# Keys kept once with two diagonal rows per key tile, and the projection products in three float32r terms, in a post-norm attention block

## What is computed

```python
qkv = x @ in_proj_weight.T + in_proj_bias          # split into q, k, v; heads of 16
qh = qh / 4
scores = einsum('bhid,bhjd->bhij', qh, kh)
rel = clip(j - i, -64, 64) + 64                    # i: query, j: key
bias = (qh @ rel_pe.T) taken at rel
attn = softmax(scores + bias)
y = layernorm(x + (attn @ vh) @ out_w.T + out_b)
out = layernorm(y + gelu(y @ binarized(w1).T + b1) @ binarized(w2).T + b2)
```

## Time and profile before

| | |
|---|---|
| median of 3 runs | 2366.7 us (2362.38 to 2367.46) |
| time of the profiled execution | 2361.56 us |
| its span, first to last instruction | 2359.6 us |
| mean granted TensorE clock | 0.978 of full speed |
| busy: PE / DVE / ACT / POOL | 94% / 74% / 67% / 46% of the span |
| projection stage, about | 0 to 217 us |
| attention stage, about | 217 to 2005 us |
| feed-forward stage, about | 2005 to 2359 us |

### The profile page before, as it was taken

How to read it: one execution, slowest core, us unless ns; L and a number is a source line. 1 busy time by engine, 2 the same in 40 slices (tenths; PEclk the granted TensorE clock), 3 DMA queues, 4 the chain that set the end, 5 groups by cost and what they waited for, 6 DMA issues and landing times. The chain is left out here.

```text
span 2359.6 us, 47824 instructions
## 1 busy us (share of the span) xinstructions
PE 2227.5 (94%) x14580; PEld 1261.9 (53%) x14580; DVE 1739.1 (74%) x3447; ACT 1573.1 (67%) x2192; POOL 1085.8 (46%) x1803
## 2 busy tenths in 40 slices
PE   8996899999999999999999999999999998899997
PEld 5563444444444444444444444444444443688886
DVE  4443777777777777777777777777777772788885
ACT  3433377777777777777777777777777776466766
POOL 1001444554445544455445545454554431567663
PEclk9998599999999999999999999999999999899999
DMA  9997777777777777777777677777777752333421
GB/s 305 400 352 265 204 208 202 210 214 211 206 207 208 208 213 209 210 203 208 212 209 212 201 208 215 209 208 202 210 213 209 209 178 73 100 102 111 111 65 45
DMA packets 334570, 468.55 MB, mean 199 GB/s; under 512 B 89797, under 2 KB 262550, under 8 KB 334486
## 3 DMA queue, kind: packets, MB, share of 16 engines
q0 software_dynamic: 120960, 215.78, 33.9%
q1 hardware_dynamic: 204358, 243.32, 32.7%
q10 hardware_dynamic: 9168, 8.52, 1.1%
HBM read 244.73 MB, written 221.25 MB: 197 GB/s over the span
## 5 line engine op out<-in xcount | busy, mean ns | idle before, releaser
L933 ACT ACTIVATE probs<-weigh_ps 128x1024 f32<-128x1024 f32 x1024 | 1048.9, 1025 | 471.8 <-PE weigh_ps L1100 468.0
L985 DVE CUSTOM_DVE_ANT_1 ring_ps<-ring_ps,band_all 128x512 f32<-128x512 f32 x1008 | 681.0, 716 | 263.8 <-PE ring_ps L1061 263.6
L1061 PE MATMUL ring_ps<-keys,queries 48*128 48x512 f32 x2048 | 827.1, 468 | 40.1 <-DVE partial_max L974 14.0
L1100 PE MATMUL weigh_ps<-queries,keys 50*128 50x512 f32 (+3 forms) x2688 | 751.0, 385 | 1.3 <-ACT probs L933 0.6
L974 DVE TENSOR_REDUCE partial_max<-ring_ps 128x2 f32<-128x1024 f32 x512 | 627.7, 1226 | 112.3 <-PE ring_ps L1061 80.8
L1061 PEld LDWEIGHTS ring_ps<-keys,queries 48*128 48x128 f32 x2048 | 370.7, 187 | 524.7 <-issue 398.9
L1117 PE MATMUL sum_ps<-probs,values 128*32 128x512 f32 x4096 | 546.6, 605 | 0.1
L839 POOL COPY carried<-carried 128x252 f32<-128x252 f32 x430 | 159.3, 396 | 568.2 <-ACT carried L922 568.2
L1085 PE MATMUL weigh_ps<-ident,band_all 128*128 128x128 f32 x2048 | 363.2, 290 | 19.3 <-ACT carried L922 16.5
L1100 PEld LDWEIGHTS weigh_ps<-queries,keys 50*128 50x128 f32 x2688 | 356.3, 186 | 14.9 <-ACT probs L933 9.5
L1085 PEld LDWEIGHTS weigh_ps<-ident,band_all 128*128 128x128 f32 x2048 | 213.6, 141 | 249.9 <-ACT probs L933 104.6
(11 more groups left out here) (119 smaller groups left out, 1857.3 us busy)
## 6 DMA issues: line engine op xcount, KB each, us to landing
band_scr<-carried SPq DMA_DIRECT2D x256, 512.0 KB, 4.8
band_all<-band_scr POOLq DMA_DIRECT2D x128, 512.0 KB, 5.4
band_all<-band_scr POOLq DMA_DIRECT2D x128, 256.0 KB, 4.4
keys<-k_scr POOLq DMA_DIRECT2D x128, 240.0 KB, 8.1
k_scr<-k_parts SPq DMA_DIRECT2D x16, 1792.0 KB, 9.8
q_scr<-q_parts SPq DMA_DIRECT2D x16, 1024.0 KB, 10.4
queries<-q_scr POOLq DMA_DIRECT2D x128, 128.0 KB, 3.8
o_scr<-weighted_s SPq DMA_DIRECT2D x64, 256.0 KB, 7.6
```

Source lines behind the costliest of these rows:

```text
L933: nc.scalar.activation(probs[:, u % PROBS], weigh_ps[weigh_of["scores", at]][:], ACT.Exp).then_inc(s_pr, 1)
L985: nc.vector.tensor_tensor_reduce(out=both, in0=both, in1=bias, scale=1.0, scalar=LOWEST, op0=ALU.add, op1=ALU.max, accum_out=partial_max[: ...
L1061: nc.tensor.matmul(dst, query_rows(c, h, ROWS, tile * P, (tile + 1) * P), key_rows(c, h, ROWS, c0, c0 + 512), start=True, stop=True, tile_ ...
L1100: last = nc.tensor.matmul(weigh_ps[weigh_of["scores", at]][:, h, e0 * P:e1 * P], key_rows(c, h, QROWS, k0, k0 + P), query_rows(c, h, QROWS ...
```

## The change

Four things are done.

1. Keys are stored once (`KCOLS` of 9 tiles in place of 15), with the left end, except tile 0's first 64 keys and the copy of tile 0 behind tile 7. A new small projection gives, for every head and query, the query times (right end minus left end): `wdT` are its weights, `d_parts` its two float32r parts, `d_scr` its DRAM copy. In `d_scr` each of six key tiles has two rows, zero except over the query tiles for which the right end applies. `load_ends` puts these 12 rows below the three terms of the queries; the keys get 12 fixed rows (`beyond`), ones where the key tile is theirs. A look product has 60 rows, a score product 62 and always 512 columns.
2. All products of the projection stage are made from two float32r parts in three terms: `wT` and `xT` have a second part, computed by DVE.
3. To make room, buffers share storage: `rel_parts` lies in `d_parts`, the incoming weights in `v_s`, the zeros in `q_parts`.
4. `d_scr` is filled with zeros by one DMA of SP, which stands behind those for `band_scr`.

The core of the diff (new left-out lines are further semaphores and the matching loads):

```diff
+    LOOK_ROWS = ROWS + ENDS * PARTS
+    QROWS = LOOK_ROWS + PARTS
-    KCOLS = (RIGHT + NT + 1) * P
+    KCOLS = (NT + 1) * P
...
+        def load_ends(eng, i, c):
+            for h in range(HG):
+                r0 = h * ROW_TILE + ROWS
+                eng.dma_start(queries[r0:r0 + ENDS * PARTS, c % SLOTS].bitcast(F32),
+                              d_scr[(i * SLOTS + c) * HG + h]).then_inc(s_d[c % SLOTS], 16)
...
+            d_parts = sb("d_parts", [H, PARTS, ENDS * P], F32R)
+            rel_parts = d_parts[:].rearrange("r c t -> r (c t)")[:, 0:PARTS * 3 * P].rearrange("r (c t) -> r c t", c=PARTS)
...
+                sp.dma_start(d_scr, over(zeros.rearrange("p n c -> p (n c)"), ENDS * PARTS, 1)).then_inc(s_zd, 16)
                 sp.dma_start(w1_s, w1.rearrange("(j p) e -> p j e", p=P)).then_inc(s_w, 16)
...
+                        act.wait_ge(s_relt, 16 * HG * TERMS)
+                        act.wait_ge(s_dout, b * 16 * PARTS + 16 * PARTS)
+                        for half in range(2):
+                            act.wait_ge(s_djob, b * 2 + (half + 1))
+                            width = min(512, ENDS * P - half * 512)
+                            nc.scalar.activation(d_parts[:, 0, half * 512:half * 512 + width], bank[half][0:H, 0:width],
+                                                 ACT.Identity, bias=bd_col[:, 0:1]).then_inc(s_dhi, 1)
...
+                for h in range(HG):
+                    r0 = h * ROW_TILE + PAD
+                    nc.vector.memset(queries[r0:r0 + PAD].bitcast(F32), 0.0).then_inc(s_zq, 1)
...
-                            if job < 4:
+                            if job < 2:
+                                pe.wait_ge(s_dlo, b * 2 + (job + 1))
+                            elif job < 4:
                                 pe.wait_ge(s_vev, b * 4 + (job + 1))
...
-                    for e0, e1 in ((0, rights), (rights, QT)):
-                        if e0 < e1:
...
+                    last = nc.tensor.matmul(weigh_ps[weigh_of["scores", at]][:, h],
+                                            key_rows(c, h, QROWS, n * P, (n + 1) * P),
+                                            query_rows(c, h, QROWS, g * 512, (g + 1) * 512),
```

More of the change, by code:

```diff
@@ L215, in post_ln_block @@
             s_xev = sem("xT_ready")
+            s_xhi = sem("xT_high_ready")
+            s_hidve = sem("weights_high_copied")
+            s_whi = sem("weights_high_ready")
+            PRODUCT = [(c, kt) for c in range(TERMS) for kt in range(KE)]
             s_vev = sem("v_ready")
@@ L289, in _ @@
                                      v_s[:, a].rearrange("p g n h d -> p g (n h d)")).then_inc(s_store[a], 16)
+                        sp.wait_ge(s_dlo, b * 2 + 4)
+                        sp.sem_inc(s_passed, 1)
+                        sp.wait_ge(s_zd, 16)
+                        for part in range(PARTS):
+                            own = d_scr[bass.ds(b * H, H), part, 0:P]
+                            sp.dma_start(flat_tiles(own, ENDS),
+                                         d_parts[:, part].bitcast(F32)
+                                         .rearrange("h (t c) -> h t c", c=P)).then_inc(s_dout, 16)
                         sp.wait_ge(s_lo, b * 8 + 16)
@@ L441, in _ @@
                             last.then_inc(s_vev, 1)
+                        for half in range(2):
+                            width = min(512, ENDS * P - half * 512)
+                            col = slice(half * 512, half * 512 + width)
+                            dve.wait_ge(s_dhi, b * 2 + (half + 1))
+                            low_part(d_parts[:, 1, col], bank[half][0:H, 0:width], d_parts[:, 0, col],
+                                     bd_col[:, 0:1]).then_inc(s_dlo, 1)
                         for m in range(2):
@@ L481, in _ @@
                 pe.wait_ge(s_dve, 1)
+                pe.wait_ge(s_block, 5)
+                for kt in range(KE):
+                    for j in range(2):
+                        nc.tensor.matmul(bank[5][:, kt * P:(kt + 1) * P], w_in_s[:, j, kt * P:(kt + 1) * P],
+                                         ends_block[:, j], start=(j == 0), stop=(j == 1))
+                pe.wait_ge(s_bias, 16)
+                for j in range(2):
+                    last = nc.tensor.matmul(bank[6][:, 0:1], ends_block[:, j],
+                                            b_col[:, j:j + 1], start=(j == 0), stop=(j == 1))
+                last.then_inc(s_wd, 1)
                 pe.wait_ge(s_wout, 16)
@@ L485, in _ @@
                 pe.wait_ge(s_evd, 2)
+                pe.wait_ge(s_wdc, 1)
                 with pe.Fori(0, B // 2) as i:
```

235 lines of the change are left out of this document (168 added, 67 removed).

## The result

The changed kernel takes 2479.99 us (median of 4 runs, 2479.3 to 2480.98) against 2365.55 us (4 runs, 2362.38 to 2367.46): ratio 1.0490, 95% interval 1.0473 to 1.0506. It is slower by 114 us, where I had forecast 20. The sign was right and the size was not.

The account below looks back on a forecast made before the run. PE was taken to bound attention, with DMA engines full in projection. Projection +24, between stages +1 and attention -5.5 gave +19.5 us, 2381 on the profiled run and 2386 us on 2366.7; range 2370 to 2400.

Parts of the forecast that it names:

- 640 pieces in all, which fall away: Attention stage: five of 16 units a step lose their split score product, columns stay; a split costs 0.04 us.
- My own test: Attention stage: the prediction counts as wrong if a step changes by more than 0.2 us; 0.09 us shorter was expected.
- Attention, -5.5: Attention stage: whole score products in place of split ones save 5.5 us, bounds 0 and 14.
- The first batch, +24.7: Projection, start: ACT waits for rel_terms behind 6.29 MB of zeros; batch 1's first product at 65.0 us, +24.7 us.
- The first rival (no stall): Projection, first batch: rel_terms overtakes the zeros or zeros are quicker, memsets set the start; 2373 us, chance 0.14.
- Were the wait gone, they would be the bound of the start: Projection, first batch: DVE's two memsets, 7.8 us, are hidden behind the rel_terms wait but would otherwise set the start.
- Batches, 23.7 us: Projection: a batch takes 18.9 us of products plus 4.8 us of waiting, 23.7 us, 0.2 us less than before.
- the 1.7 us of the sum: Projection: the gain claimed over seven batches from each taking 0.2 us less.
- The rival of the clock: Projection: the clock falls in every batch, 1.5 us more for seven batches, +10; 2396 us, chance 0.12.
- Between the stages, +1: Between projection and attention: SP's stores wait for POOL instructions and two more DMAs; +1 us, bounds 0 and +4.

Follow-up runs that it names:

- run 5: Changed kernel plus 24 one-column products (96 PE instructions) behind PE's last transpose of the projection stage; 2384.18 us, ratio 1.0097.
- run 6: Changed kernel with run 5's 24 products, and the zero fill of d_scr issued behind the loads of rel_terms; 2375.86 us, ratio 1.0057.
- run 8: As run 6, with DVE's two memsets of the queries' rows also moved to POOL behind its last load of x; 2374.62 us, ratio 1.0053.
- shift 96, before: Kernel before the change with 96 semaphore increments ahead of PE's first wait, moving its later instructions 96 places; 2440.17 us, ratio 1.0323.
- shift 16, after: Changed kernel with 16 PE instructions (one-column products) added behind the last transpose of the projection stage; 2505.31 us, ratio 1.0597.

## Why the prediction was wrong, and where it was right

- **The missing term.** The step that failed is the one on attention, "640 pieces in all, which fall away": I priced fewer instructions by what each took on PE and never asked where the loop would stand; a fetch of instructions was not a term of the sum at all. In place of -5.5 us the stage measured +93.2. The fetch costs 98.5 us (1878.4 in the changed kernel, 1779.9 with the same loop shifted by 96), 7.0 for each of the 14 back edges: 3.5 at the edge itself (49.6 / 14), the rest at the second block and by the clock, which stood at its half for 85 us behind the first pass and for none of it when shifted. My own test, a step that changes by more than 0.2 us, was the one that fired: 6.6 us over four steps. It could have been suspected: both programs' counts of instructions were to be had, and the trace of before showed one fetch for each block and none after the first pass. Which of the two sides of the limit it would fall on needed x, and no view gave that. So a rival for a loop that is fetched again, with a chance of its own, was what was called for; its price no row of before could give.
- **Attention, -5.5.** With the stalls gone the stage is 5.3 us shorter (1785.2 against 1779.9), a pass 107.3 in place of 107.75 us, 0.11 us a step; I had 0.09. Right. The score pieces had no run of their own, so that the gain is theirs is argued, not shown.
- **The first batch, +24.7.** Measured +24.0 (64.30 against 40.32), ACT, transposes and first product each within 0.7 us. Only PE's own work ended at 51 where I had 48, as the memsets took 2 x (3.47 + 0.91) us where I had 7.8 for both and as the clock was low at the start; under the wait that cost nothing. Taken apart, from the 63.84 of run 5: 9.7 us are the wait (54.15 in run 6), 6.2 more the memsets (47.99 in run 8), and 7.7 are left for the later start, the rest of the wait and the clock. The first rival (no stall) was wrong on its ground: the loads did not overtake the zeros. The estimate of 4.3 us for a memset from the Trainium skill (VectorE: DVE Perf Modes, "Zero memsets can be issued as uint32 (trn2)": one cycle for each element) is nearer to the measured 3.47 + 0.91 us than the mean that I took from rows.
- **"Were the wait gone, they would be the bound of the start"**: wrong. Run 8 took both away and gained 1 us over run 6. The bound is the full DMA queue: the store of batch 0's differences, behind 6.3 MB of zeros, 2 MB of weights and the stores of keys and values.
- **Batches, 23.7 us.** At the full clock they are 23.45 us apart (186.06 to 209.51), before 23.94. In three of the six after batch 1 the clock fell for 3.4 us behind PE's wait of 2.55 us, and the two of these whose length shows took 24.9 and 25.0. So the seven batches did not win the 1.7 us of the sum but cost 1.2 more than before (first product of batch 1 to the end of the last: 165.8 in place of 164.6). The rival of the clock was half right: 1.5 us each as priced, in half of the batches.
- **Between the stages, +1.** The stage moved by 25.2 and the end of the last products by 25.2 too (204.89 to 230.07): nothing.
- Without the fetch the time is 2384 us (run 5) against 2386 forecast. That it comes so near is in part luck: the batches were 2.9 us too cheap in the sum, the first batch and the step between the stages 2.7 us too dear. The large terms were sound; one was missing.

## What to carry to other kernels

When a change adds or removes instructions of an engine that runs a long hardware loop, count where the loop begins and ends in blocks of 256 instructions, before and after, and look for q8 in a window of its later passes: 0 or as many as the loop has blocks and one more. A few instructions put where the engine stands anyway move it back; make room for that before a change is judged, or a gain of 5 us in a stage reads as a loss of 93. And of a wait at the head of a full queue ask what is behind it in the same queue, as that is what one gets when it is gone.

## What was unexpected of the hardware

- A loop of 1633 instructions of PE that lies in eight blocks is fetched anew in every pass (9 packets of 16 KB), one of 1713 in seven only once. Each pass loses 4.7 us (shift 96, before) to 8.8 us (shift 16, after; 8.7 with 20).
- PE's semaphore increments stand 0.151 us apart; a weight load and a one-column product together take 0.116 us (5.59 us for 48 pairs, granted clock 0.96). To shift a loop, products are the cheaper filling by 2.6 to 1 for each instruction.
- PE's half clock followed each stall of some 4 us within the loop and lasted 3.4 to 10.2 us (up to 13.7 with a shift of 16, where PE stands twice), so a stall costs more than its own length: 7.0 us a pass where the back edge shows 3.5.
